# Three attention layers' projections with full-height weight rows, and input, stores and output moved across stage borders

## The reference

```python
B, T, D, E, H = (4, 256, 128, 4, 8)   # setup; x here is (4, 1024, 128)
def _layernorm(x, w, b):
    mu = jnp.mean(x, axis=-1, keepdims=True)
    var = jnp.mean(jnp.square(x - mu), axis=-1, keepdims=True)
    return (x - mu) * jax.lax.rsqrt(var + EPS) * w + b
```

## Time and profile before

| what | us |
|---|---|
| runs | 3286.0, 3297.26, 3285.5 (median 3286.0) |
| the profiled execution | 3277.16 |
| its span, first to last instruction | 3275.1 |
| TensorE busy | 2907.9 (89%) |
| VectorE busy | 2459.1 (75%) |
| ScalarE busy | 2215.6 (68%) |
| GpSimd busy | 188.5 |
| mean granted TensorE clock | 0.917 |

### The profile page before, as it was taken

The page is one execution under the profiler, slowest core; times in us unless marked ns, Lnnn a source line. Parts: engine busy times, 40 slices in busy tenths (PEclk is TensorE's granted clock), DMA queues, the critical chain, the costliest instruction groups (busy, mean ns, idle before and its releaser), DMA issues. The chain is left out here.

```text
span 3275.1 us, 53109 instructions
## 1 busy us (share of the span) xinstructions
PE 2907.9 (89%) x19734; PEld 1664.7 (51%) x19734; DVE 2459.1 (75%) x3887; ACT 2215.6 (68%) x3872; POOL 188.5 (6%) x329
## 2 busy tenths in 40 slices
PE   6868999859999999977999989799997777789998
PEld 4643444422333333353444456678885455578886
DVE  5648999479999999747999564477776777677776
ACT  2345888638888888953888722288886444378886
POOL 0030000020000000030000020100000000010000
PEclk9957999869999999966999989799998888889999
DMA  1052121030000000033221010211110000111112
GB/s 28 1 114 64 29 40 21 6 106 11 21 21 21 21 21 21 2 83 84 41 41 21 2 28 1 66 40 46 46 49 21 1 0 0 39 50 46 49 46 58
DMA packets 76838, 115.24 MB, mean 35 GB/s; under 512 B 13840, under 2 KB 38448, under 8 KB 76592
## 3 DMA queue, kind: packets, MB, share of 16 engines
q1 hardware_dynamic: 76592, 111.99, 14.5%
HBM read 85.73 MB, written 25.43 MB: 34 GB/s over the span
## 5 line engine op out<-in xcount | busy, mean ns | idle before, releaser
L797 DVE TENSOR_REDUCE nested_a_halves<-banks 128x2 f32<-128x1024 f32 x512 | 617.4, 1222 | 78.8 <-PE banks L896 75.6
L849 ACT ACTIVATE nested_a_p<-banks 128x512 f32<-128x512 f32 x1024 | 553.7, 597 | 117.1 <-PE banks L926 100.7
L797 DVE TENSOR_REDUCE wide_a_halves<-banks 128x2 f32<-128x1024 f32 x512 | 593.4, 1216 | 42.1 <-PE banks L896 42.1
L849 ACT ACTIVATE wide_a_p<-banks 128x512 f32<-128x512 f32 x1024 | 554.1, 598 | 44.5 <-PE banks L926 33.2
L1725 DVE TENSOR_TENSOR mix_e_h_low<-mix_e_h,mix_e_h_high 128x512 fp32r<-128x512 f32 x512 | 349.6, 688 | 174.9 <-ACT mix_e_h_high L1831 167.0
L1848 ACT ACTIVATE mix_e_h<-banks,mix_b_folded 128x512 f32<-128x512 f32 x512 | 353.8, 691 | 103.5 <-PE banks L1902 103.1
L939 PE MATMUL banks<-nested_a_p,nested_values 128*32 128x256 f32 x4096 | 326.9, 398 | 0.0
L939 PE MATMUL banks<-wide_a_p,wide_values 128*32 128x256 f32 x4096 | 321.0, 391 | 0.0
L1831 ACT ACTIVATE mix_e_h_high<-mix_e_h 128x512 fp32r<-128x512 f32 x512 | 319.3, 624 | 0.0
L896 PE MATMUL banks<-nested_k_stack,nested_q_stack 48*128 48x512 f32 x1024 | 270.8, 524 | 48.8 <-PEq L453 24.3
L926 PE MATMUL banks<-nested_q_stack,nested_k_stack 50*128 50x512 f32 x1024 | 252.3, 423 | 10.9 <-ACT nested_a_p L849 9.9
(11 more groups left out here) (365 smaller groups left out, 4190.2 us busy)
## 6 DMA issues: line engine op xcount, KB each, us to landing
mix_e_gate<-mix_gates_t SPq DMA_DIRECT2D x128, 256.0 KB, 3.2
nested_q_stack<-nested_q_parts SPq DMA_DIRECT2D x96, 128.0 KB
nested_q_parts<-nested_p_q_cut SPq DMA_DIRECT2D x16, 512.0 KB
nested_k_parts<-nested_p_k_cut SPq DMA_DIRECT2D x16, 512.0 KB
nested_k_stack<-nested_k_parts SPq DMA_DIRECT2D x32, 256.0 KB
wide_q_stack<-wide_q_parts SPq DMA_DIRECT2D x192, 32.0 KB
nested_k_stack<-nested_k_parts SPq DMA_DIRECT2D x32, 128.0 KB
mix_raw_w<-L_ffn_w_t SPq DMA_DIRECT2D x8, 512.0 KB, 7.2
```

The costliest lines, as they stand in the source:

```text
L797: dve.tensor_reduce(halves[:, half, i, 2 * a:2 * a + 2], bank[:, at:at + 2, :], AX, ALU.max).then_inc(maxed, 1)
L849: act.activation(p[:, kt % 4, j, :], bank[:, ST + n % RING, :], ACT.Exp, scale=scale).then_inc(probs, 1)
```

## The change

- The load block issues sequence 0 only and waits for nothing; the causal stage issues sequences 1 to 3 behind its weights. VectorE waits for sequence 0 at its start and for the others behind the second row maximum.
- Nested projections use four copies of each weight, with the rows past 128 >> e set to zero; ScalarE makes them by a copy scaled with a 0/1 column (`keep_rows`; six copies before h is copied, three after, three for wo later). Every product then has 128 rows.
- The row factor of the nested projection and of the mixture's front is one power of one affine function of the variance; the other factors of the nested layer follow one sequence later (`other_factors`).
- TensorE turns sequence b+1 between the q and k products and the value products of sequence b; VectorE normalises b+2 before the last cut; ScalarE cuts the high parts before it copies the next h, and grows x behind that.
- SyncE's order in the projection: weights, store 0, store 1, load 0, store 2. In the attention block: load 1, first shift rows, store 3, load 2, and so on. Each load waits for the parts of its own sequence; ScalarE waits for none.
- The last mixture stores each chunk of x (256 KB) itself: `store_chunk(c-1)` before the gates of expert 6 of chunk c, the last at the end. The store block is gone.

```diff
-            for b in range(B):
-                sp.dma_start(core.x[:, b * TILES:(b + 1) * TILES, :],
-                             x_dram[b].rearrange("(i p) d -> p i d", p=P)).then_inc(x_in, 16)
-            sp.wait_ge(x_in, 16 * B)
+            load_sequence(core, sp, x_dram, 0)
...
+    def store(self, sp, b, n):
+
+        dram = (self.q_parts, self.k_parts)[n]
+        for part in range(self.parts):
+            dst = dram[b * self.groups:(b + 1) * self.groups, :, :, part].rearrange("g s h e t -> (g s h) e t")
+            sp.dma_start(dst, self.plain(self.cuts[n][:, b % 2, part, :])).then_inc(self.parts_out[b % 2], 16)
+
     def load(self, sp, n):
 
-        k = n % self.SLOTS
+        b, k = n // self.groups, n % self.SLOTS
+        sp.wait_ge(self.parts_out[b % 2], (b // 2 + 1) * 32 * self.parts)
...
                 store(0)
                 store(1)
                 sp.wait_ge(ones_set, hd.SLOTS)
-                sp.wait_ge(parts_out[0], 32 * hd.parts)
-                for n in range(2):
-                    hd.load(sp, n)
-                for b in range(2, B):
+                hd.load(sp, 0)
+                for b in range(2, B - 1):
                     store(b)
...
+                def first_factor(b):
+
                     power = core.minus_half[:, 0:TILES]
+                    scale, floor = (1.0 + LN_EPS, LN_EPS * LN_EPS) if masked else (1.0, LN_EPS)
+                    dst = both if masked else rstd
                     pool.wait_ge(counted, (b + 1) * STATS)
...
+                    pool.tensor_scalar(padded[:, b], moments[:, b, :, 1], scale, floor, ALU.mult,
+                                       ALU.add).then_inc(factored, 1)
+                    pool.wait_ge(factored, b * FIRST + 1)
+                    pool.tensor_tensor(dst[:, b], padded[:, b], power, ALU.pow).then_inc(factored, 1)
...
+                def keep_rows(weight):
+
+                    for e in range(1, 4):
+                        act.activation(weight[:, e, :], weight[:, 0, :], ACT.Copy,
+                                       scale=core.keep[:, e:e + 1]).then_inc(kept, 1)
+
...
+                if masked:
+
+                    for weight in (wq, wk):
+                        keep_rows(weight)
                 copy_turned(0)
-                copy_turned(1)
+                if masked:
+                    keep_rows(wv)
                 for b in range(B):
+                    for n in range(2):
+                        cut_high(b, n)
+                    if b == 1 and masked:
+                        act.wait_ge(hd.wo_in, 16)
+                        keep_rows(hd.wo)
+                    if b + 1 < B:
+                        copy_turned(b + 1)
                     if masked:
                         grow_rows(b)
...
                                 last = pe.matmul(bank[:, 2 + 2 * n + c, (lo - 4 * c) * P:(hi - 4 * c) * P],
-                                                 weight[0:m, :], h_t[0:m, b % 2, lo * P:hi * P], start=True, stop=True)
+                                                 weight[:, e, :], h_t[:, b % 2, lo * P:hi * P], start=True, stop=True)
                             last.then_inc(projected, 1)
+                    if b + 1 < B:
+                        turn(b + 1)
...
-                for k in range(2):
-                    sp.wait_ge(hd.parts_out[k], 16 * hd.parts * B)
-                hd.load(sp, 2)
+                hd.load(sp, 1)
                 for u in range(UNITS):
                     shift_load(u)
+                    if u == 0:
+
+                        for n in range(2):
+                            hd.store(sp, B - 1, n)
+                        hd.load(sp, 2)
...
+                def store_chunk(c):
+
+                    sp.wait_ge(added, c + 1)
+                    dst = out_dram[c // 2, c % 2 * BANK:(c % 2 + 1) * BANK].rearrange("(i p) d -> p i d", p=P)
+                    sp.dma_start(dst, x[:, c * 4:(c + 1) * 4, :]).then_inc(stored, 16)
```

171 lines of the change are left out of this document (81 added, 90 removed).

## The result

The changed kernel takes 3178.9 us (median of 4 runs, 3171.9 to 3185.5) against 3291.6 us of the kernel before on the same chip: a ratio of 0.9655, with a 95% interval of 0.9621 to 0.9690, 113 us less. A second set of four runs gave 3172.7 us and 0.9621 (0.9601 to 0.9641). The forecast was 3206 us, with 3186 as the low end: right in sign and in that full rows bring the clock, 27 us short in size.

The account below looks back on a forecast made before the run. It took the seams as the bound: start, projections at low clock with SyncE's transfers behind them, mixture starts, end. Terms -6.4 -28 -25.5 -12.5 +1 -2.4 -6 sum to -80 us, giving 3206 us; range 3186 to 3238.

Parts of the forecast that it names:

- -6.4 forecast: Kernel start: with only sequence 0 awaited, VectorE starts near 5 us instead of 11.4, saving 6.4 us.
- The end, -6 forecast: Kernel end: the last chunk is stored straight after the last add, without the block barrier, saving 6 us.
- With a clock that flickers as in wide I take 10 us: Nested projection: each sequence takes 10 us with full rows, the clock behaving as in the wide projection.
- the two ends that "meet": End of nested1's projection: compute done at 216 us, load 0 landed near 214, so 217 instead of 245.0.
- rival (d): Nested projections: transfers set the attention start, 5.8 MB taking 41 us; 8 us a layer lost, 3220 us; chance 0.04.
- My large end, "a full clock": Nested projections: full clock and ScalarE's 8.4 us per sequence save 33 us in nested1, 30 in nested2.
- rival (b): Nested projections: clock does not answer to rows, 31 us less saved, 3237 us; chance 0.26 together with a late-rising clock.
- Small end: Nested projections: clock stays at 0.50 and only the gap before attention is saved, 12.7 and 10 us.
- is 9.1 us, from 661 on: Wide projection: VectorE's work per sequence, counted from 661 us, toward attention starting near 700.3 and 12.5 us saved.
- My range of -9.9 to -15: Wide projection: from only SyncE's overhang going (-9.9) to no landing wait (-15), around -12.5 us.
- +0.5 each: Nested attention: stores queued ahead of unit 1's shift rows cost 0.5 us per layer, +1 us in all.
- the -1.2 forecast: Start of each mixture layer: a shorter GpSimd chain saves 1.2 us, limited by the first weight transfer.

Follow-up runs that it names:

- old_engine_orders: Changed kernel with the old order of turns, cuts, growing and normalising on TensorE, ScalarE and VectorE; 3210.7 us, 0.9789 of the kernel before.
- full_rows_only: Kernel before with only the nested q, k and v products put on 128 rows by zeroed weight copies; 3277.8 us, ratio 0.9963.
- narrow_rows: Changed kernel with nested q, k and v products on the rows in use alone (128, 64, 32, 16); 3210.5 us, 0.9762 of the kernel before.
- warm_both: Changed kernel plus 16 filling products before the nested scores and one wide product ahead of each of 48 score products; 3272.3 us, 0.9957 of the kernel before.
- new_sync_only: Kernel before with only the new SyncE transfer order and without the waits for all stores; 3252.4 us, ratio 0.9907.
- old_sync_order: Changed kernel with loads 0 and 1, then stores 2 and 3, back in the projection block; 3221.8 us, 0.9795 of the kernel before.
- ten_steps: Changed kernel with both powers again: ten GpSimd steps in nested projections, five in the mixture front; 3194.3 us, 0.9693 of the kernel before.
- half_rows: Changed kernel with nested q, k and v products on at least 64 rows instead of 128; 3199.7 us, 0.9716 of the kernel before.

## Why the prediction was short

**Start and end.** -6.4 forecast, -6.2 to the first statistics (11.40 to 5.24). The end, -6 forecast, -7.0: 3.4 us from add to end of span, where I had summed 4.4.

**Nested projection.** That full rows bring the clock was right. The step that failed is "With a clock that flickers as in wide I take 10 us": a pace read from a stage in which TensorE waits was put down to the clock, and the new orders of the engines got no term but the earlier first product. With full rows and the old orders a sequence does take 10.0 us at a clock of 0.82 (old_engine_orders; 9.9 in full_rows_only). With the new orders it takes 8.0 at 0.88, mostly because TensorE idles 2.0 us in the stage and not 6.6. TensorE's own work per sequence was also 6.9 us (27.65/4), where I had 8 to 9.

In nested1 TensorE's last product therefore ends 39.4 us into the stage, not 49.2 (212 less the start): 0.7 us of that from a first product at 9.8 and not 10.6, the rest from the sequences. Behind it work goes on for 9.6 us, not 4; 3.30 of them are the landing of store 1, which I had counted in wide alone. The last 0.6 us, which I had at 1, are the border. That leaves the 4.6 us (4.8 in nested2) by which the stages beat the forecast. The other of the two ends that "meet" moved too: I had load 0 landed 51.2 us into the stage (214), and it let the scores go at 49.6, so less work behind TensorE's last product would have gained no more. From the first store (171.0 us) to that landing it is 34.5 us, not the 41 of rival (d). My large end, "a full clock", -33 and -30, agrees with the -32.6 and -30.3 by luck as much as by reason: the clock was not full, and the last sequence cost 5.6 us that are not in it.

That the rows are the cause, the point of rival (b), was settled for the forecast: narrow_rows brings back a clock of 0.53, and costs 31.4 us in the two stages where rival (b) had 31. The Trainium skill, page TensorE: Matmul & The Clock Gate, section Part 1: The HAM clock gate, ties the gate to how busy the engine has been. Here TensorE was busy 98 to 100% of the time at 0.50 to 0.54 in narrow_rows, in warm_both and in the earlier trace rows; the measurement decides.

**Small end and rival (b) taken as additive.** I worked out the value of the rows as 31 us and of SyncE's gap as 22.7 us, as if one could be had without the other. The sum holds only for both together: full_rows_only gave 9.4 us in the two layers, new_sync_only 22.0, the whole change 62.9. No error in the total came of it, but any forecast for half of the change would have been wrong.

**Wide projection.** The step that failed is that VectorE's work per sequence "is 9.1 us, from 661 on": it kept the start at which TensorE had been let go in the kernel before, and nearly its pace. The turn of sequence 1 no longer stands ahead, so the first q product moved from 14.1 to 8.6 us, and a sequence takes 8.0 us instead of 9.6. The last work ends 44.9 us into the stage, where it was 54.3 before and I had 51 (699). old_engine_orders puts the orders at 9.5 us and old_sync_order the gap at 10.2; together 19.7 for the 18.8 gained, so here the two do add up. My range of -9.9 to -15 gave the orders no term of their own. It also charged 2 us for the landing of store 1, and VectorE waited 0.48 us there.

**Attention.** "+0.5 each" was to be the stores in front of the shift rows; no such wait is in the trace, and that part held. What came instead had no term: -1.7 and -1.6 us from the output products, which now have 128 rows (missed), and from the clock -2.0 us in the first step and -5.1 in the tail of nested1, +3.9 and -0.6 in the first two steps of nested2. Only the output products can be put down to the change; the other 3.9 us net lie within what the stages of one and the same kernel differ by.

**Mixtures.** TensorE's folds start 9.1 us into mix2 before and 7.8 us after the earlier trace rows, the -1.2 forecast; they wait 1.71 us for the first weights, as the step said:

```profile
2763.80 3.55 PE L1924 MATMUL banks<-mix_shift,mix_raw_w 128*128 128x1 f32 x16 [1.71 <-DMA mix_raw_w<-L_ffn_w_t]
```

ten_steps puts them back to 9.1 us in both mixtures, so it is the one power that brings this. In mix1 the folds gained 1.7 us, and the stage 0.2: something later in it took the rest back, and I did not look for it.

**The sum.** The span gained 24.9 us more than the 80 forecast: 9.4 in the nested projections, 6.3 in the wide one, 3.3 in the two output stages, 3.9 net from the clock in the nested attention, 1.0 for the stores that cost nothing there, 0.5 at the start and 2.7 in mix2 and the end, less 2.1 in the layers between. The low end of the range failed since the three largest terms came out at or past their large ends together, and they share a cause: the new orders let the first sequence's products start earlier and take TensorE's waits out of each sequence (10.0 us become 8.0 in nested1, 9.6 become 8.0 in wide), and I had carried that through for the first product of the nested stages only.

## What to carry to other kernels

Where a stage ends with the later of two paths (products on one engine, transfers on another), price both parts of a change together and each alone: here 5.5 and 12.3 us alone, 32.6 together with the new orders. When a step ahead of the first product is taken away, redo the whole chain from the new start, and do not carry over a pace that was read with the old order of work. And when TensorE is busy and its granted clock is low all the same, look at how many rows its products use: here the copies with zero rows took ScalarE 2.0 us ahead of the first product of a nested stage, and full rows brought 31.4 us in the two stages.

## What was not expected of the hardware

- A TensorE that never idles can stay at 1.2 GHz: 53.5 us at 0.53 in narrow_rows, 90 us in warm_both. With 64 rows at the least, one layer stayed at 0.50 for 55 us, and its twin was at 1.00 over 21 us of its projecting.
- Narrow products are not only a matter of clock. Eight products of 256 columns take 1.89 us with 128 rows each (changed kernel at 169 us, clock 0.98), and 2.19 us with 128 and 64 rows in turn (nested2 of half_rows, clock 1.00); in the output stage sixteen take 2.19 us narrow and 1.86 on 128 rows, both at 1.00. The rows:

```profile
1397.18 2.19 PE L724 MATMUL banks<-nested_p_h_t,nested_p_wq 128*128 128x256 f32 x8
```

```profile
636.21 2.19 PE L1048 MATMUL banks<-nested_wo,nested_o_m_t 128*128 128x128 f32 x16
```

```profile
589.57 1.86 PE L1077 MATMUL banks<-nested_wo,nested_o_m_t 128*128 128x128 f32 x16
```

- The clock can fall to 0.50 in the last two units of an attention stage, for 12 to 25 us, in one execution and not in the next; it cost 5.1 to 5.3 us, twice 9.5. Why is open.
